# DLRM forward pass on one core: the output layer with h4 as stationary side, moved behind the next chunk's first strip, and two stacks moved ahead of t4's strips

## The reference

```python
fm = emb_table[jnp.arange(26)[None, :], cat_idx]            # 26 tables of 12500 x 128
h = relu(dense_x @ Wd1 + bd1)                                # 13 -> 512
h = relu(h @ Wd2 + bd2); dense = relu(h @ Wdf + bdf)         # -> 256 -> 128
Z = concatenate([fm, dense[:, None, :]], axis=1)             # 27 vectors of 128
S = einsum('bie,bje->bij', Z, Z); interactions = S[:, iu, ju]  # 351 pairs
x = concatenate([interactions, dense], axis=-1)              # 479 wide
x = relu(x @ Wt1 + bt1); x = relu(x @ Wt2 + bt2)             # 1024, 1024
x = relu(x @ Wt3 + bt3); x = relu(x @ Wt4 + bt4)             # 512, 256
return sigmoid(x @ Wo + bo)                                  # 2048 x 1
```

## Time and profile before

| | us |
|---|---|
| median of 3 runs | 631.34 |
| lowest and highest run | 623.7 and 631.71 |
| the profiled execution's own time | 631.94 |
| its span, first to last instruction | 629.9 |
| PE busy | 571.2 (91% of the span) |
| POOL busy | 403.5 (64%) |

### The profile page before, as it was taken

One profiled execution on the slowest core, in us unless ns is written; L12 is line 12 of the kernel. 1 busy time (PEld: TensorE's weight loads), 2 busy tenths in 40 slices (PEclk: granted clock), 3 DMA queues, 4 the chain that ended last, 5 costly groups with the idle time before them and its releaser, 6 DMA issues.

```text
span 629.9 us, 18067 instructions
## 1 busy us (share of the span) xinstructions
PE 571.2 (91%) x8112; PEld 538.4 (85%) x8112; DVE 211.7 (34%) x438; ACT 241.0 (38%) x506; POOL 403.5 (64%) x421
## 2 busy tenths in 40 slices
PE   0997279989798999999998999999999999999998
PEld 0775268989697899999998999999999999999987
DVE  6763434523341224231431234122423142214111
ACT  1774423534342334242432344243424343424222
POOL 6777777777777777777777777777777776000000
PEclk9999659989999999999998999999999999999999
DMA  6645637893349443774368433953386336500530
GB/s 126 165 108 107 181 55 250 283 351 55 56 84 292 118 57 54 216 225 55 53 158 284 55 56 53 310 133 56 52 251 190 57 53 189 201 3 2 190 145 0
DMA packets 36309, 83.93 MB, mean 133 GB/s; under 512 B 8086, under 2 KB 23966, under 8 KB 30678
## 3 DMA queue, kind: packets, MB, share of 16 engines
q0 software_dynamic: 13312, 27.29, 26.4%
q1 hardware_dynamic: 22360, 55.30, 25.1%
q10 hardware_dynamic: 562, 0.20, 0.2%
HBM read 74.37 MB, written 8.40 MB: 131 GB/s over the span
## 4 chain that ended last, share of the span: by engine, by line
PE 72%; POOL 13%; DMA 6%; issue 6%; DVE 2%; ACT 1%; DVEq 0%
PE acc L715 57%; POOL gathered L491 13%; PE bank L747 7%; PE unit L764 5%; DMA wt<-split_t 5%; PE acc L725 1%; PE unit L778 1%; DMA gathered<-table,row_of 1%; ACT h L626 1%; DVE h L553 0%; ACT acc L627 0%; DVE feats L572 0%; DVE feats L499 0%; DVE rows L572 0%; DVE feats L498 0%
## 5 line engine op out<-in xcount | busy, mean ns | idle before, releaser
L491 POOL DMA_INDIRECT gathered<-table,row_of x416 | 402.8, 968 | 129.6 <-issue 126.4
L715 PE MATMUL acc<-h,wt 128*128 128x256 f32 (+1 forms) x2568 | 344.7, 291 | 11.3 <-DVE h L553 5.1
L715 PEld LDWEIGHTS acc<-h,wt 128*128 128x128 f32 x2568 | 321.6, 193 | 19.5 <-DVE h L553 8.7
L626 ACT ACTIVATE h<-acc,bias 128x256 fp32r<-128x256 f32 (+1 forms) x104 | 51.1, 491 | 246.6 <-PE acc L715 246.6
L553 DVE TENSOR_TENSOR h<-acc,h 128x256 fp32r<-128x256 f32 (+1 forms) x104 | 46.3, 445 | 284.6 <-ACT acc L627 269.6
L715 PE MATMUL acc<-x,wt 126*128 126x256 f32 (+2 forms) x768 | 97.1, 286 | 1.5 <-DVE h L550 1.3
L715 PEld LDWEIGHTS acc<-x,wt 126*128 126x128 f32 (+2 forms) x768 | 94.0, 193 | 5.2 <-issue 3.1
L747 PE MATMUL bank<-eye,gathered 128*128 128x128 f32 x416 | 53.9, 280 | 11.7 <-ACT feats L659 7.9
L764 PE MATMUL unit<-feats 128*27 128x26 f32 x4096 | 52.0, 194 | 9.5 <-issue 7.2
L764 PEld LDWEIGHTS unit<-feats 128*27 128x27 f32 x4096 | 44.0, 107 | 19.3 <-issue 8.3
L659 ACT ACTIVATE feats<-bank 128x512 f32<-128x512 f32 (+1 forms) x56 | 55.9, 1094 | 9.8 <-PE bank L747 9.6
(11 more groups left out here) (44 smaller groups left out, 170.5 us busy)
## 6 DMA issues: line engine op xcount, KB each, us to landing
wt<-split_t SPq DMA_DIRECT2D x35, 1024.0 KB
raw<-w_t SPq DMA_DIRECT2D x17, 512.0 KB
split_t<-wt SPq DMA_DIRECT2D x8, 1024.0 KB, 10.9
gathered<-table,row_of POOLq DMA_INDIRECT x416, 3.4
raw<-w_d SPq DMA_DIRECT2D x1, 512.0 KB
feats<-xT SPq DMA_DIRECT2D x4, 104.0 KB
rows<-idx SPq DMA_DIRECT2D x1, 208.0 KB, 2.5
raw<-w_df SPq DMA_DIRECT2D x1, 128.0 KB
```

What stands on the lines that cost most here:

```text
L491: nc.gpsimd.indirect_dma_start(gathered[:, t % SLOTS, c, :], None, table, bass.IndirectOffsetOnAxis(row_of[:, t, c:c + 1], 0)).then_inc(ga ...
L626: nc.scalar.activation(parts[0], source, ACT.Relu, bias=b)
L715: mm = nc.tensor.matmul(result, strip[0:height, a, k, :], given[0:height, b, k, :], start=(n == 0 and (a, b) == (0, 0)), stop=(n == len(bl ...
```

## The change

Five things change. The output layer uses `h4` as the stationary side: for each half of 128 samples and each of the two blocks, one matmul with 128 x 128 of h4 stationary and one column of `wo_s` moving, into two columns of `bank` 3 (which it shares with the flips, so that the first flip of the next tile waits for the sigmoid). The result stands on 128 partitions, so `bo_s` is repeated over them, `y` becomes [128, 8, 2], and the store writes 4-byte pieces. `out` has counters of its own and leaves the accumulator ring. The step is moved behind the first t1 strip of the following part; the last part's stays at the end. And in parts 2 to 6 the second tile's flips go one place forward (13 and 14), its pairs too (15 to 18), both regroups stand at 19, stack 0 at 20 and stack 1 at 21. Parts 0 and 1 keep their places.

```diff
--- before.py
+++ after.py
@@ -146,39 +146,45 @@
 
 
 
-NEXT_AT = [(6, 8, 9, 10, 11, 12, 14, 15, 16, 17, 18, 19, 20, 21, 22, 22) for _ in PARTS]
+NEXT_AT = [(6, 8, 9, 10, 11, 12, 13, 14, 15, 16, 17, 18, 19, 19, 20, 21) for _ in PARTS]
 
 NEXT_AT[0] = (9, 10, 12, 13, 14, 15, 19, 20, 21, 22, 22, 22, 22, 22, 22, 22)
 NEXT_AT[1] = (8, 9, 10, 11, 12, 13, 15, 16, 17, 18, 19, 20, 21, 21, 22, 22)
+
+
+def out_of(part):
+
+    number = PARTS.index(part)
+    return [(1, [("out", PARTS[number - 1])])] if number else []
 
 
 def mixed(part, following):
     strips = strips_of(part, "t1", "t2", "t3", "t4")
     steps = [[s] for s in features(following, 0) + features(following, 1) + regroups(following)] + stacks(following)
-    inserted = list(zip(NEXT_AT[part[0] // CHUNK], steps))
+    inserted = out_of(part) + list(zip(NEXT_AT[part[0] // CHUNK], steps))
     if part == PARTS[0]:
 
         places = [2 * m + 1 for m in range(T2_SLOTS)] + [9 + m for m in range(8 - T2_SLOTS)]
         inserted += [(n, piece("t2", m)) for m, n in enumerate(places)]
-    return woven(strips, *inserted) + [("out", part)]
+    return woven(strips, *inserted)
 
 
 STEPS = first_part()
 for one, following in zip(PARTS, PARTS[1:]):
     STEPS += mixed(one, following)
-STEPS += strips_of(PARTS[-1], "t1", "t2", "t3", "t4") + [("out", PARTS[-1])]
+STEPS += woven(strips_of(PARTS[-1], "t1", "t2", "t3", "t4"), *out_of(PARTS[-1])) + [("out", PARTS[-1])]
 
 HALVES = {"flip": (range(0, 4), range(4, len(FLIPS))), "regroup": (range(0, 2), range(2, len(REGROUPS)))}
 
 
-KINDS = ("spread", "stack", "acc", "split", "piece", "bank", "unit", "tile", "dense")
+KINDS = ("spread", "stack", "acc", "split", "piece", "bank", "unit", "tile", "dense", "out")
 
 
 def counts(step):
     kind = step[0]
     split = kind in ("spread", "stack") or (kind == "strip" and step[2] not in ("df", "t4"))
     return {"spread": int(kind == "spread"), "stack": int(kind == "stack"),
-            "acc": int(kind in ("strip", "out")), "split": int(split),
+            "acc": int(kind == "strip"), "out": int(kind == "out"), "split": int(split),
             "piece": int(kind == "piece"),
             "bank": len(HALVES[kind][step[-1]]) if kind in HALVES else 0,
             "unit": int(kind == "pair" and step[4] == 1), "tile": int(kind == "flip" and step[-1] == 1),
@@ -288,9 +294,9 @@
         eye = sb("eye", [P, P])
         bias = sb("bias", [P, BIASES])
         wo_s = sb("wo_s", [P, 2])
-        bo_s = sb("bo_s", [1, 1])
+        bo_s = sb("bo_s", [P, 1])
         row_of = sb("row_of", [P, TILES, CATS], U32)
-        y = sb("y", [1, CHUNK])
+        y = sb("y", [P, len(PARTS), CHUNK // P])
 
 
         split_t2 = nc.dram_tensor("split_t2", (8, P, 2048), F32, kind="Internal").ap()
@@ -328,6 +334,7 @@
         spread_high = sem("spread_high")
         stack_high = sem("stack_high")
         acc_read = sem("acc_read")
+        out_read = sem("out_read")
         high_dense = sem("high_dense")
         odd_bank_read = sem("odd_bank_read")
         odd_unit_read = sem("odd_unit_read")
@@ -335,6 +342,7 @@
         spread_done = sem("spread_done")
         stack_done = sem("stack_done")
         acc_done = sem("acc_done")
+        out_done = sem("out_done")
         bank_done = sem("bank_done")
         unit_done = sem("unit_done")
 
@@ -343,6 +351,8 @@
         feats_flat = feats[:].rearrange("p g s j -> p (g s j)")
         wide_x_raw, wide_w_raw = feats_flat[:, 0:B], feats_flat[:, B:B + 512]
         stacks_in = [unit[:, b].rearrange("p (h w) -> p h w", h=2) for b in range(2)]
+
+        out_sums = bank[:, 3, 0:CHUNK // P]
         products = [unit[:, u, 0:UNIT * CATS].rearrange("p (g i) -> p i g", i=CATS) for u in range(2)]
 
         kept_rows = prods[:].rearrange("p i g -> p (i g)")[:, 0:TILES * CATS].rearrange("p (t c) -> p t c", c=CATS)
@@ -596,7 +606,7 @@
                 act.dma_start(wide_w_raw[32 * q:32 * q + CONT + 1], w1).then_inc(wide_in, 16)
             act.wait_ge(constants_in, 16 * 4)
 
-            nc.scalar.activation(y[0:1, 0:1], bo_s[0:1, 0:1], ACT.Sigmoid)
+            nc.scalar.activation(y[:, 0, 0:1], bo_s[:], ACT.Sigmoid)
 
             for at, step in enumerate(STEPS):
                 kind, now = step[0], SO_FAR[at]
@@ -626,13 +636,13 @@
                         nc.scalar.activation(parts[0], source, ACT.Relu, bias=b)
                         nc.scalar.activation(source, source, ACT.Relu, bias=b).then_inc(acc_read, 1)
                 if kind == "out":
-                    part = step[1][0] // CHUNK
-                    if part:
-                        act.wait_ge(y_out, 16 * part)
-                    nc.scalar.activation(y[0:1, :], result_at(step, number)[0:1],
-                                         ACT.Sigmoid, bias=bo_s[0:1, 0:1]).then_inc(acc_read, 1)
-                    act.wait_ge(acc_read, number + 1)
-                    act.dma_start(out[columns(step)].rearrange("b o -> o b"), y[0:1, :]
+
+                    part = now["out"]
+                    act.wait_ge(out_done, part + 1)
+                    nc.scalar.activation(y[:, part, :], out_sums, ACT.Sigmoid, bias=bo_s[:]).then_inc(out_read, 1)
+                    act.wait_ge(out_read, part + 1)
+                    act.dma_start(out[columns(step)].rearrange("(h p) o -> p (h o)", p=P), y[:, part, :],
+                                  allow_slow_non_contiguous=True
                                   ).then_inc(y_out, 16)
                 if kind == "rest":
 
@@ -721,11 +731,18 @@
 
                     h4_at = max(n for n in range(at) if STEPS[n][0] == "strip" and STEPS[n][2] == "t4")
                     pe.wait_ge(acc_read, SO_FAR[h4_at + 1]["acc"])
-                    for k in range(2):
-                        mm = nc.tensor.matmul(result[0:1], wo_s[:, k:k + 1], h4[:, k, :],
-                                              start=(k == 0), stop=(k == 1))
-                    mm.then_inc(acc_done, 1)
+
+                    pe.wait_ge(even_bank_read, upto(now["bank"], odd=False))
+                    pe.wait_ge(odd_bank_read, upto(now["bank"], odd=True))
+                    for h in range(CHUNK // P):
+                        for k in range(2):
+                            mm = nc.tensor.matmul(out_sums[:, h:h + 1], h4[:, k, h * P:(h + 1) * P], wo_s[:, k:k + 1],
+                                                  start=(k == 0), stop=(k == 1))
+                    mm.then_inc(out_done, 1)
                 if kind in HALVES:
+                    if kind == "flip" and now["out"] and step[2:] == (0, 0):
+
+                        pe.wait_ge(out_read, now["out"])
                     if kind == "regroup":
 
                         pe.wait_ge(even_unit_read, upto(now["unit"], odd=False))
@@ -803,7 +820,7 @@
         "w_t1": np.concatenate([t1, np.zeros_like(t1[0:1]), np.asarray(L0_rec_bt1)[None]])[X_ROWS], "w_t2": L0_rec_Wt2, "w_t3": L0_rec_Wt3, "w_t4": L0_rec_Wt4,
         "biases": biases.T,
         "wo": np.asarray(L0_rec_Wo).reshape(2, P).T,
-        "bo": np.asarray(L0_rec_bo).reshape(1, 1),
+        "bo": np.repeat(np.asarray(L0_rec_bo).reshape(1, 1), P, axis=0),
     }
     given = {k: np.ascontiguousarray(v) for k, v in given.items()}
     nc = bacc.Bacc("TRN2", target_bir_lowering=False, num_devices=1)
```

## The result

| | us |
|---|---|
| changed kernel, median of 20 runs (630.09 to 637.65) | 632.75 |
| kernel before, median of 20 runs (623.7 to 635.91) | 629.27 |
| ratio of the two, 95% interval | 1.0062, 1.0041 to 1.0083 |
| profiled execution of the changed kernel: own time, span | 632.1, 629.6 |
| predicted | 626.9 (620.5 to 633.0) |

The change makes the kernel slower by 0.6% (0.4 to 0.8), where I forecast a gain of 0.7%. The time lies inside the range, near its end, and it does so because the range was wide: the direction is wrong. The kernel before came to 629.27 over 20 runs, not to the 631.34 of three, so the execution that I read (631.94) stood 2.7 us above its kernel's median.

What follows compares the result with a forecast made beforehand. TensorE was taken as full from part 1 on. Terms -0.35 - 2.05 + 1.5 - 3.89 + 0.4 = -4.4 us took the profiled 631.94 to 627.5; as that execution stood 0.6 above the median, forecast 626.9, range 620.5 to 633.0.

Steps and rivals of the forecast that it cites:

- The output layer turned round: Mid-kernel output layer with h4 stationary: 0.90 us a part for 0.95, seven times, -0.35 us.
- a pair serial: Rival: output layer's weight loads do not hide, 0.325 us a pair, 13.6 us above forecast, 640.5 us; chance 0.06.
- Placement behind strip 0: Output layer behind t1's first strip: the wait for h4 and leaving the accumulator ring cost nothing.
- The stacks in parts 2 to 6: Regroups ahead of t3's last strip remove the 0.41 us idle before the stacks, five times: -2.05 us.
- The spare 0.12 us at t4's fourth block: t4's first strip needs t3's low half after 1.58 us; ready at 1.46, so no wait, by 0.12 us.
- Parts 0 and 1: Stacks stay last and lose the output layer's cover, so t1 waits: twice 0.74, +1.5 us.
- The flips one place forward: Flips ahead of strip 13 cover late reloaded weights: -3.13 us in part 3, -0.76 in part 4, -3.89 together.
- waits for gathers: Rival: gathers become the bound, the second tile's flip waits 1.6 us, about 628.8 us in all; chance 0.07.
- such waits come and go: Rival: waits for reloaded weights only move to another strip, so 3.9 us stay, 630.8 us; chance 0.18.
- The end: Last part's output layer and store: +0.4 us together, with +0.7 for the store in 4-byte pieces, bounds 0 and +6.

Runs made afterwards that it cites:

- `e6_row_late_old_at`: Changed kernel with the output layer as one row, contiguous store, and the kernel before's places for all other steps: 633.42 us, ratio 1.0064 to the kernel before.
- the run with all rows: Changed kernel's order of steps, output layer put back to one row with a contiguous 1 KB store: 627.21 us, ratio 0.9979 to the kernel before.
- the best version: Changed kernel with row form and contiguous store in the last part only, second tile's steps in parts 0 and 1 packed closer: 623.99 us, ratio 0.9895.
- `e3_row_pieces`: Kernel before, its row of 256 results still on one partition but stored in 256 pieces of 4 bytes: 634.19 us, ratio 1.0105.
- `e7_new_at_only`: Kernel before with only the new places of parts 2 to 6, output step in row form at each part's end: 632.88 us, ratio 1.0069.

## Why the prediction was wrong, step by step

- **The output layer turned round**: -0.35 us foretold; 0.81 us a part in place of 0.95, so seven times is -1.0. The term was right in kind and priced a little too dear. The rule of the Trainium skill, TensorE: Matmul & The Clock Gate, Part 3, that a weight load overlaps a running matmul only where the row groups differ, would have made a pair serial; 0.101 us a pair against 0.325 contradicts it on full rows.
- **Placement behind strip 0**: free, as said; the row at 307.07 has no wait, and ACT's store issue (0.38 us) delays nothing that TensorE waits for.
- **The stacks in parts 2 to 6**: -2.05 us foretold, and the gap is gone in every one of them. The spare 0.12 us at t4's fourth block was not there, which costs 0.11 us five times; against that, the eight stack transposes hold TensorE for 0.71 us in two groups of four where I had 0.99. So the term holds about as it stood.
- **Parts 0 and 1**: 0.74 us each foretold, 0.89 measured in part 1. With all seven boundaries in that state the kernel loses 2 to 6 us (`e6_row_late_old_at`).
- **The flips one place forward** (-3.89 us foretold): this term failed. The wait in part 3 was real, and the cover works, but I took one execution's waits, and the 1.5 us that its slower clock added in part 3, as the kernel's. In four profiles with the old places the waits are 3.3, 2.9, 1.7 and 0.2 us, and with the flips forward waits for gathers, 1.2 us in the mean, stand in their place, a cost that the sum put at nothing. The edit alone gives +0.2% (-0.1 to +0.5). Over 29 to 32 runs the kernel before scatters from 623.6 to 638 us, and twelve of the fourteen profiles have stops or waits of 1 to 4 us in the stretch of t2 in parts 1 to 3, some with a slower clock behind them. My own text said that such waits come and go and gave that 0.18; it should have been the forecast. The hint was there: the lowest of three runs, 623.7, lay 8 us under the profiled one.
- **The end** (+0.4 us foretold): this is the step that turned the sign. The store took 8.1 us, not 2.2. I had written that no row shows such a store and gave it bounds of 0 and +6, and then chose +0.7 "near the gathers' lower end", though gathers write SBUF in rows of 512 bytes and this writes DRAM in pieces of 4. The runs show that it is the pieces' size; they don't show why small pieces are slow to report, nor whether pieces that lie far apart in DRAM would be.

Put together with what was measured: -1.0 - 2.05 + 2 x 0.89 + 0 + 6.4 (6.6 of landing less 0.2 of sigmoid) = +5.1 us; measured is +3.5 by the medians and +3.9 (2.6 to 5.2) by the ratio. The two errors, 3.9 and 6.0 us, had the same sign. What remains, 1.2 to 1.6 us, is within the scatter and was not pursued.

The Trainium skill, DMA: Bandwidth & Descriptors (Rules for kernel authors), says one descriptor per element where the last dimension is not contiguous. The trace agrees, with 270 more packets a store. The same page's opening table puts the least transfer for full rate at 512 bytes, with a read-modify-write below it. The runs agree that small writes are dear, but between 4 and 32 bytes they show a step of 6 us and between 32 bytes and 1 KB one of 0.6, so most of this price lies far below that size.

## What to carry to other kernels

Ask of each transfer whether anything runs beside it. The same store in pieces costs nothing measurable seven times in the middle and all of its landing time the eighth time, at the end. The layout of a last store decides more than the engine work in front of it, so give the last block the layout that stores in whole rows, even where all others have another.

And before a wait in one profile becomes a term of the sum, ask whether the runs shown scatter by as much as the term. If they do, its mean is not known, and undoing it may only move it.

## What was unexpected of the hardware

Writes to DRAM in pieces of 4 bytes are reported landed 7 to 8 us after the issue, whether there are 256 or 128, from one partition or 128; in pieces of 8 bytes it takes 3.5 us, of 32 bytes 2.1, and as one row 1.5. With 256 pieces the DMA engines are busy for only half a microsecond of it.

TensorE stops in t2 without waiting for a semaphore, in the middle of a group, in most cases while the DMA engines are near full (a share of 0.87 in the stretch below). In the run with all rows:

```profile
335.95 4.51 PE L726 MATMUL acc<-h,wt 128*128 128x256 f32 x23 [2.00 <-issue]
...
336.00:340.00 4.00, 4.00 (x21) 4.00 (x22) 0.00 (x0) 0.00 (x0) 3.09 (x4) 0.57 0.87 327
```

and in the best version:

```profile
202.92 0.20 PE L791 MATMUL unit<-feats 128*27 128x26 f32 x1 [3.26 <-issue]
```

Each of these two stops is followed by some 3 us at a granted clock near 0.5, the level of 1.2 GHz; the first costs 3.4 us in this way, 2.00 of stop and 1.4 in the strip. That doesn't follow from a stop's length here: behind stops of 2.41 us (the kernel before, at 205.66), 2.10 (`e3_row_pieces`, at 330.60) and 2.35 (`e7_new_at_only`, at 335.38) the clock stays at 1.00.

One such stop, of 1.9 to 2.9 us, comes at the same instruction in all fourteen profiles, ahead of the last 3 products of a pair in part 0, near 129 us; those of parts 1 to 3 come and go. What causes them no run here tested. There is a hint. The page of the kernel before lists a DMA queue of the kind `instruction`, with 64 packets of 16 KB over the whole span:

```profile
q8 instruction: 64, 1.05, 0.7%
```

In all fourteen profiles one of its packets is under way during the stop near 129 us, and in 11 of the 14 stops of 1 us or more in parts 1 to 3 as well, though a packet takes only about 1 us and comes each 10 us. That the two come together is no proof of a cause, and it stays open.
